# Mamba block, cross attention and gated feed-forward in one kernel: attention work handed to GpSimd, an earlier start of the attention, and four small edits at the ends

## What is computed

```python
x = _layernorm(x + _L0_attn_ref(x, in_proj_w, conv_w, conv_b, dt_bias, A_log, D, norm_w, out_proj_w))
x = _layernorm(x + _L0_xattn_ref(x, ctx, ctx, 0, mask))
x = _layernorm(x + _L0_ffn_ref(x, W_gate, W_up, W_down))
```

```python
scores = einsum('bsgrd,btgd->bgrst', xq, xk) / sqrt(16) + mask      # 8 key heads, 4 queries each
out = einsum('bgrst,btgd->bsgrd', softmax(scores), xv)
h = silu(x @ W_gate.T) * (x @ W_up.T);  out = h @ W_down.T
```

## Time and profile before

| | us |
|---|---|
| median of 3 runs | 1634.29 |
| the profiled execution | 1632.67 |
| its span | 1630.9 |
| PE busy | 1609.1 |
| ACT / DVE / POOL busy | 945.8 / 1192.2 / 975.8 |

### The profile page before, as it was taken

The page is one execution under the profiler, slowest core; times in us unless marked ns, Lnnn a source line. Parts: engine busy times, 40 slices in busy tenths (PEclk is TensorE's granted clock), DMA queues, the critical chain, the costliest instruction groups (busy, mean ns, idle before and its releaser), DMA issues.

```text
span 1630.9 us, 25574 instructions
## 1 busy us (share of the span) xinstructions
PE 1609.1 (99%) x9096; PEld 1268.2 (78%) x9096; DVE 1192.2 (73%) x2370; ACT 945.8 (58%) x1578; POOL 975.8 (60%) x741
## 2 busy tenths in 40 slices
PE   9999999999999999999999999999999999989998
PEld 7788888888888888888888888888888885444646
DVE  7767687767877686868685868586858689996443
ACT  6765377446835583648373837383728565994231
POOL 4977478656956594849493949385938573331000
PEclk9999999999999999999999999999999999999999
DMA  5432133212412231314231414132404245000000
GB/s 206 143 104 82 55 105 135 78 60 92 135 59 91 87 129 56 104 59 136 69 114 45 136 59 136 46 116 79 136 13 136 91 86 129 1 21 20 16 12 26
DMA packets 73570, 138.83 MB, mean 85 GB/s; under 512 B 6786, under 2 KB 10882, under 8 KB 73092
## 3 DMA queue, kind: packets, MB, share of 16 engines
q1 hardware_dynamic: 73444, 137.21, 26.2%
HBM read 132.98 MB, written 2.63 MB: 83 GB/s over the span
## 4 chain that ended last, share of the span: by engine, by line
PE 92%; DVE 5%; issue 1%; DMA 1%; ACT 0%; POOL 0%; SPq 0%; DVEq 0%; POOLq 0%; ACTq 0%
PE ps_hs L249 8%; PE ps_hs L251 8%; PE ps_hs L250 8%; PE ps_gate L250 8%; PE ps_gate L249 8%; PE ps_gate L251 8%; PE ps_y L1220 7%; PE ps_hs L1229 7%; PE ps_hs L1230 7%; PE ps_hs L1228 7%; PE ps_gate L1204 4%; PE ps_y L1513 3%; PE ps_hs L1438 3%; PE ps_dec L1438 3%; DVE pr L1052 2%
## 5 line engine op out<-in xcount | busy, mean ns | idle before, releaser
L799 DVE SCALAR_TENSOR_TENSOR conv<-ps_hs,cw,conv 128x508 f32<-128x508 f32 (+2 forms) x432 | 320.0, 741 | 31.5 <-ACT conv L566 20.3
L400 POOL TENSOR_TENSOR cum_bc<-cum_bc,neg_cum 128x1024 f32<-128x1024 f32 x128 | 247.5, 1934 | 10.8 <-DMA cum_bc<-cum_scratch 0.2
L249 PE MATMUL ps_hs<-x_hi,w_hi 128*128 128x512 f32 x576 | 231.5, 402 | 0.0
L251 PE MATMUL ps_hs<-x_hi,w_lo 128*128 128x512 f32 x576 | 225.2, 391 | 0.0
L249 PE MATMUL ps_gate<-x_hi,w_hi 128*128 128x512 f32 x576 | 224.4, 390 | 0.0
L250 PE MATMUL ps_hs<-x_lo,w_hi 128*128 128x512 f32 x576 | 224.4, 390 | 0.0
L250 PE MATMUL ps_gate<-x_lo,w_hi 128*128 128x512 f32 x576 | 224.3, 389 | 0.0
L251 PE MATMUL ps_gate<-x_hi,w_lo 128*128 128x512 f32 x576 | 224.2, 389 | 0.0
L1228 PE MATMUL ps_hs<-wo_hi,g_hi 128*128 128x512 f32 x488 | 190.5, 390 | 0.0
L1230 PE MATMUL ps_hs<-wo_hi,g_lo 128*128 128x512 f32 x488 | 190.0, 389 | 0.0
L1229 PE MATMUL ps_hs<-wo_lo,g_hi 128*128 128x512 f32 x488 | 190.0, 389 | 0.0
(11 more groups left out here) (177 smaller groups left out, 3327.6 us busy)
## 6 DMA issues: line engine op xcount, KB each, us to landing
cum_bc<-cum_scratch SPq DMA_DIRECT2D x128, 512.0 KB, 4.1
w_raw<-w_in SPq DMA_DIRECT2D x145, 256.0 KB, 4.6
wo_raw<-w_out SPq DMA_DIRECT2D x64, 256.0 KB, 4.8
g_acc<-x_t SPq DMA_DIRECT2D x4, 512.0 KB, 5.6
acc<-x_nat SPq DMA_DIRECT2D x1, 2048.0 KB, 9.2
out<-y_out SPq DMA_DIRECT2D x8, 256.0 KB, 2.0
wg_sb<-w_gate SPq DMA_DIRECT2D x1, 1792.0 KB, 7.0
wu_sb<-w_up SPq DMA_DIRECT2D x1, 1792.0 KB, 11.0
```

The source lines that it names most:

```text
L249: eng.matmul(ps, whi, xhi, start=(k == 0), stop=False)
L251: return eng.matmul(ps, wlo, xhi, start=False, stop=(k == n - 1))
L400: gp.tensor_tensor(part, part, start.broadcast_to([P, 2, HB, SEQ]), ALU.add).then_inc(S["bc_ok"], 1)
L799: v.scalar_tensor_tensor(out=dst, in0=src, scalar=cw[:, at, TAPS - 1 - n:TAPS - n], in1=dst, op0=ALU.mult, op1=ALU.add).then_inc(S["tap"], 1)
```

## The change

- **POOL's share.** For `par` 1 a new `less_max(i)` on POOL takes the row's extreme from the four tiles at once, in place, and ACT takes their exponential in one instruction of 128x512 instead of four of 128x128. The add of `att` to `acc` moves from DVE to POOL (`add_attended(n)`). The copy out of the turned `par` 1 tiles is DVE's for even chunks and ACT's for odd ones (`keep_turned_too`).
- **Earlier beginning.** Each batch's last products have a bank of their own. Only batches 0 to 2 are finished ahead of `turn_queries(0)`; batches 3 to 7 are cut in quarters (one or two of the four tiles) that stand between the first chunks. Batch 0 is normalized alone, batch 1 through POOL's `powers`, and DVE's parts of batches 3 to 7 stand between `masked` calls.
- **Loads.** `v_raw` is issued behind the six key copies; POOL's copy of it to `v_ext` stands behind the second `k_bd`.
- **Ends.** POOL waits for the eight prefix sums before it splits the third weight tile; the variances of the second norm come in three calls of `powers`; the last batch's down products are made in two halves of 256 columns, in banks of their own, and DVE adds and measures them half by half.

The core of the diff:

```diff
-        LAST_PS = ps_hs + ps_gate + ps_dec + ps_gate
+        LAST_PS = ps_hs + ps_dec + ps_gate + ps_y
@@ SP: the v_raw load moved behind the six key copies
@@ POOL, beginning
+            pool.wait_ge(S["dt_dve"], 2 + BATCH)
             split(2)
@@ POOL, attention
+            def add_attended(n):
+                b, o = n // 2, n % 2
+                pool.wait_ge(S["att_ok"], n + 1)
+                cols = slice(o * 256, (o + 1) * 256)
+                gp.tensor_tensor(acc[:, b, cols], acc[:, b, cols], att[:, o, :], ALU.add).then_inc(S["xa_ok"], 1)
+            def less_max(i):
+                pool.wait_ge(S["s_max"], 2 * i + 2)
+                part = pr[i % 3][:, REP:2 * REP, :]
+                gp.tensor_tensor(part, part, neg_max[:, i % 3, REP:2 * REP].unsqueeze(2).broadcast_to([P, REP, SEQ]),
+                                 ALU.subtract).then_inc(S["sub_ok"], 1)
             for i in range(CHUNKS):
                 need(pool, S["s_ps"], 2 * i - 2)
                 gp.tensor_tensor(k_bd[i % 2][:, :, :],
...
+                if i == 1:
+                    powers(1, 0, slice(1, 2))
+                    pool.wait_ge(S["v_ones"], 1)
+                    wait_alone(pool, S["v_in"], 16)
+                    gp.tensor_copy(v_ext[:, :, :, 0:AD], v_raw[:, :, :].rearrange("p b (g d) -> p b g d", d=AD))\
+                        .then_inc(S["v_ok"], 1)
...
+                if i >= 2:
+                    less_max(i - 2)
...
+                if i % 2 == 0 and i >= 10:
+                    add_attended((i - 10) // 2)
+            less_max(CHUNKS - 2)
+            less_max(CHUNKS - 1)
+            for n in range(CHUNKS // 2 - 5, 2 * BATCH):
+                add_attended(n)
             pool.wait_ge(S["acc_ok"], BATCH * GROUPS)
             pool.wait_ge(S["o_ps"], 2 * BATCH * GROUPS)
             for m in range(MT):
                 wait_alone(pool, WD_IN[m % 2], 16 * (m // 2) + 16)
                 gp.tensor_copy(wd_sb[:, m, :], wd_raw[:, m % 2, :]).then_inc(S["wd_ok"], 1)
-            powers(2, slice(HB, BATCH))
+            powers(2, 2, slice(HB, BATCH))
@@ ACT
+                if par:
+                    act.wait_ge(S["sub_ok"], i + 1)
+                    part = pr[i % 3][:, REP:2 * REP, :].rearrange("p r t -> p (r t)")
+                    sc.activation(part, part, ACT.Exp, scale=-1.0).then_inc(S["p_exp"], 1)
+                    return
...
+                if i >= 4 and i % 2 == 0:
+                    keep_turned_too(i - 3)
@@ DVE, attention
+            FIRST_PARTS = {0: (3, 4), 1: (5,), 2: (6,), 4: (7,)}
             for i in range(CHUNKS + 3):
-                if i >= 3:
+                if i >= 3 and (i - 3) % 2 == 0:
                     keep_turned(i - 3)
...
@@ DVE, feed-forward
                     if m == 0:
                         attended(BATCH - 1, 0)
+                    if m == 1:
+                        batch_done(BATCH - 2)
                     if m == 2:
+                        attended(BATCH - 1, 1)
+                    if m == 3:
                         batch_done(BATCH - 1)
                     if m == 4:
-                        dve.wait_ge(S["pow2"], 2)
+                        dve.wait_ge(S["pow2"], 3)
@@ PE, first chunks
             turn_queries(0)
-            pe.wait_ge(S["gacc_ok"], kept + 3)
-            last_products((6,), range(TPH))
-            pe.wait_ge(S["rstd_v"], GROUPS)
+            last_products((3,), (0, 1))
+            pe.wait_ge(S["gacc_ok"], kept + 2)
             scores(0)
-            pe.wait_ge(S["gacc_ok"], kept + 4)
-            last_products((7,), range(TPH))
-            pe.wait_ge(S["v_ok"], 1)
-            pe.wait_ge(S["gacc_ok"], kept + 6)
+            last_products((3,), (2, 3))
+            turn_queries(1)
+            last_products((4,), (2, 3))
+            pe.wait_ge(S["gacc_ok"], kept + 4)
+            scores(1)
+            last_products((5,), (2, 3))
+            rest = {1: (6, (0, 1)), 2: (6, (2, 3)), 3: (7, (0, 1)), 4: (7, (2,)), 5: (7, (3,))}
@@ PE, the last batch's down products
+                    if n == BATCH - 1:
+                        for c in range(2):
+                            cols = slice(c * HID // 2, (c + 1) * HID // 2)
+                            for m in range(MT):
+                                for part, hh in enumerate((h_hi, h_lo)):
+                                    mm = pe.matmul(ps_gate[c][:, cols], hh[:, m, b * SEQ:(b + 1) * SEQ],
+                                                   wd_sb[:, m, cols],
+                                                   start=(m == 0 and part == 0), stop=(m == MT - 1 and part == 1))
+                            mm.then_inc(S["dn_ps"], 1)
+                        continue
```

143 lines of the change are left out of this document (81 added, 62 removed).

## The result

The changed kernel takes 1642.14 us (median of 6 runs, 1641.19 to 1643.15) against 1634.04 us for the kernel before in the same comparison (6 runs, 1632.42 to 1634.81): ratio 1.0052, 95% interval 1.0042 to 1.0063. It is slower by 8.1 us; forecast was 1640, range 1633.5 to 1645.5. The profiled execution took 1642.63 us, its span is 1640.5.

The account below looks back on a forecast made before the run. PE was taken as the bound, busy 1609.1 of 1630.9 us. 1632.67 - 1.4 (start) - 5.5 (attention) + 11.0 (stall) + 2.0 (clock) - 0.2 (last batch) = 1638.6 profiled, median 1640.2; range 1633.5 to 1645.5.

Parts of the forecast that it names:

- The stall: Feed-forward's norm: POOL's powers queue behind the down-weight conversions, DVE and then PE wait; 11.0 us lost (9.5 to 11.5).
- The clock: Feed-forward, after PE's long wait: the granted clock falls to half and the way back costs 2 us (0 to 2.9).
- The attention's beginning: Up to chunk 10: fewer products ahead of scores(0), but 4.9 us of PE waits; change of -0.7 us (-3 to +2).
- The rest of the attention: Behind chunk 10: ACT and DVE relieved, PE becomes the bound, 1.2 of 7.4 us of waits left; 6.2 us gained.
- The start: Prefix sums without POOL's split beside them: PE's waits of 1.19 and 0.21 us go; 1.4 us gained (0 to 1.4).
- The last batch: Last batch's down products in halves: shorter DVE add and statistics against more matmuls; net 0.2 us gained (-4 to +0.6).
- The rule on the shared ports: DVE with two SBUF inputs and POOL block each other; bears only on five first_part at the start, up to 1 us each.

Follow-up runs that it names:

- p1_powers: The changed kernel with POOL's last powers moved from behind the fourteen down-weight conversions to behind the second: 1629.86 us, 0.9976 of the kernel before.
- p6_vfirst: p1_powers with the values' load issued ahead of the six key copies again, as in the kernel before: 1629.69 us, 0.9975 of before.
- p5_cover: p1_powers with products of batch 3's second two tiles ahead of scores(0) and batch 1's inverse root made earlier on POOL: 1629.19 us, 0.9972 of before.
- p2_oldbegin: p1_powers with the attention's beginning (order of products, DVE's parts, normalization of batches 0 and 1) as in the kernel before: 1626.19 us, 0.9955 of before.
- p10_copies: p2_oldbegin with DVE's early masks and row statistics reordered, and two late copies of turned probabilities moved from DVE to ACT: 1625.65 us, 0.9953 of before.
- p3_start: The kernel before with only POOL's wait for the prefix sums ahead of its weight split added: 1631.87 us, 0.9988 of before.
- p7_dveadds: p2_oldbegin with the sixteen adds of att on DVE again instead of POOL: 1629.83 us, 0.9977 of before.

## Why the prediction was right, point by point

- **The stall, +11.0 forecast, 10.30 measured, shown.** The mechanism was the one named: conversions paced by a buffer of two, queued ahead of the powers on POOL, DVE waiting in order, PE behind it. p1_powers took it out with one statement and gained 12.3 us with the clock. The term was 0.7 too large (its own readings, 1511.9 in place of 1500.7, even make 11.2): it put two norms and an `h_f`, 1.7 us, between the powers and PE, but PE needed only the first of the norms and went on 0.69 us after DVE had begun it. The conversions took 18.95 us where 19.0 was forecast.
- **The clock, +2.0 forecast, about 1.7 there.** The feed-forward is 12.0 us longer than in p1_powers, of which the wait is 10.30. The granted clock was at 0.50 behind it, the lower level of 1.2 GHz, until some point between 1510 and 1512 (0.61 in that window).
- **The attention's beginning, -0.7 forecast, about -3.0, the far end of its range: the step that failed.** Chunk 10's scores come at 1396.09 where before they came at 1393.05, from the same mark. Two things of that step were wrong. "Unhindered by the values' load I guess them 2 to 3 us earlier": they came no earlier (the first `k_bd` at 1359.61, before 1359.58), and p6_vfirst shows the two loads' order to be worth nothing. My lower bound of 0 was the value. So PE waited 2.91 us where I had put 0.4. And I had priced a falling clock only for the long stall; it fell behind this short one too, which stretches what comes next (the scores' 1.56 us in place of 1.13, the products 0.42 us apart in place of 0.227). The second weighs more. PE's waits up to chunk 10 sum to 0.96 + 2.91 + 0.28 + 1.39 = 5.5 us where I had 4.9 in all, since what was too low ahead of `scores(0)` was too high behind it; of the 2.3 us that the step is off, 0.6 are waits and some 1.6 are left for the clock. That DVE's parts stand in a chain behind it was right in kind (p5_cover: cover given at one place comes back at the next). p2_oldbegin puts the price of the early beginning at 2.2 us by the traces and 3.7 by the medians.
- **The rest of the attention, 6.2 forecast, about 5.4.** From chunk 10's scores to the first hidden product it was 77.7 us before and 72.3 after. PE became the bound at 11.87 us a batch. Of the 7.4 us of waits, 3.0 stayed where I had left 1.2; p10_copies shows that the relief of DVE does not reach them. POOL's subtraction takes 1.04 us in the steady part (I took 1.2), the add 0.73 (0.65). In a batch DVE is busy for 10.68 us (forecast 10.6), ACT for 11.31 (10.9), POOL for 9.71 (10.3).
- **The start, 1.4.** p3_start: 1.7 us between the medians; its ratio's interval, 0.9979 to 0.9997, is 0.5 to 3.4 us. Right in place and size, within what can be told.
- **The last batch, 0.2.** By the trace 0.26; the runs cannot tell it from nothing.
- **The sum.** 12.0 lost in the feed-forward (the last batch's 0.2 is already in it), 2.4 gained in the attention, 1.4 to 1.7 at the start: 7.9 to 8.2 net against 8.1 measured. The forecast had 5.5 gained in the attention and 12.8 lost in the feed-forward: two errors of 3.1 and 0.8 that partly cancel. That 1640 lay as near to 1642 as it did is to that extent luck.
- **The rule on the shared ports.** The prediction named one add of two SBUF tiles on DVE (L1075, once in two chunks), which the change takes off DVE, and left it at that. p7_dveadds puts it back beside the subtraction: 764 ns instead of 430. The Trainium skill, "SBUF — State Buffer", section "SBUF: two separate sides", says that a VectorE operation with two SBUF inputs and a GpSimd operation that reads SBUF lock each other out for a whole instruction; the trace agrees: 0.33 us more in the mean on each add, and the end of each that is drawn out lies 0.27 to 0.29 us behind the subtraction's. So it is not enough to count an add at its old price: giving POOL the subtraction made the adds dearer, and moving both was worth 3.6 us more by the medians than moving one (2.7 in the lengths of the attention). That the one instruction waits for the other is in the traces; that ports are the reason is the skill's, and no run of mine separates them from another cause.

## What to carry to other kernels

An in-order queue that gets a new duty late in a stage moves everything behind it: before moving work to an idle engine, list what that engine still has to do behind the new wait, and who waits for that; here one statement's place was worth 12 us, more than all the intended gains together. Work that covers a load can't be taken away to start sooner unless the load itself comes sooner; price the uncovered wait with the clock behind it, and subtract the waits that a slower PE no longer has. Relief of an engine whose instructions wait for the helper's, as DVE's adds do here, has to be counted as a set, not operation by operation.
